# Fetching a batch's expert rows beside the attention rounds, and a routing chain spread over more gates: a two-layer transformer on one core

## What is computed

```
x = x + L0_attn(layernorm(x))   # differential attention, 16 heads of 8
x = x + L0_ffn(layernorm(x))    # 8 experts of 512, top 2 of 8, capacity 1280 rows an expert
x = x + L1_attn(layernorm(x))   # causal attention, 16 heads of 64
x = x + L1_ffn(layernorm(x))    # 8 experts of 64, top 4 of 8, and a shared one of 256
```

## Time and profile before

| | |
|---|---|
| median of 3 runs | 1513.7 us (1513.47 to 1518.37) |
| the profiled execution | 1500.44 us, span 1499.2 us |
| PE busy | 1437.6 us, 96% of the span |
| DVE, ACT, POOL busy | 1074.6, 951.5, 745.5 us |
| mean granted PE clock | 0.994 of full speed |

### The profile page before, as it was taken

The page is one execution under the profiler, slowest core; times in us unless marked ns, Lnnn a source line. Parts: engine busy times, 40 slices in busy tenths (PEclk is TensorE's granted clock), DMA queues, the critical chain, the costliest instruction groups (busy, mean ns, idle before and its releaser), DMA issues.

```text
span 1499.2 us, 26266 instructions
## 1 busy us (share of the span) xinstructions
PE 1437.6 (96%) x8801; PEld 856.5 (57%) x8801; DVE 1074.6 (72%) x3430; ACT 951.5 (63%) x2448; POOL 745.5 (50%) x1260
## 2 busy tenths in 40 slices
PE   4999999999989999979999999999999999998999
PEld 2434443444438889855565655656565565655666
DVE  5899999999944777547677687777767777674333
ACT  4588888887884334436767677676767777673221
POOL 7334656665455633633636365454636444353322
PEclk9999999999999999989999999999999999999999
DMA  7266655556334665720000000000000000020421
GB/s 142 57 159 134 143 141 148 110 106 150 113 131 165 213 211 190 256 64 1 15 1 15 1 12 5 3 14 1 16 2 14 3 1 2 2 58 1 99 76 52
DMA packets 70600, 113.39 MB, mean 76 GB/s; under 512 B 18857, under 2 KB 35114, under 8 KB 70458
## 3 DMA queue, kind: packets, MB, share of 16 engines
q0 software_dynamic: 33104, 61.73, 16.9%
q1 hardware_dynamic: 36928, 49.19, 10.9%
q10 hardware_dynamic: 434, 0.79, 0.2%
HBM read 71.86 MB, written 39.91 MB: 75 GB/s over the span
## 4 chain that ended last, share of the span: by engine, by line
PE 79%; DVE 10%; ACT 6%; issue 2%; POOL 1%; DMA 1%; SPq 0%; ACTq 0%; DVEq 0%; POOLq 0%
PE pS L1391 10%; PE bank L1424 9%; PE bank L1404 8%; PE bank L1235 6%; PE pS L1206 4%; PE bank L1433 4%; PE pS L1310 4%; PE bank L1376 4%; PE bank L1324 4%; PE bank L1361 4%; PE pS L1311 4%; PE bank L1372 3%; DVE mx L1831 3%; ACT ar L1561 3%; PE bank L1472 3%; PE bank L1226 2%
## 5 line engine op out<-in xcount | busy, mean ns | idle before, releaser
L2535 POOL TENSOR_SCALAR ar<-ar,rd 128x512 f32<-128x512 f32 (+3 forms) x512 | 269.3, 540 | 325.9 <-DVE rd L2266 324.0
L1831 DVE TENSOR_REDUCE mx<-pS 128x1 f32<-128x512 f32 x512 | 326.3, 677 | 19.4 <-PE pS L1206 17.6
L1651 ACT ACTIVATE ar<-ar,nm 128x512 f32<-128x512 f32 (+3 forms) x512 | 285.9, 560 | 83.1 <-DVE nm L2257 82.4
L2257 DVE CUSTOM_DVE_ANT_0 ar<-pS,maskf 128x512 f32<-128x512 f32 (+3 forms) x512 | 227.3, 481 | 6.3 <-PE pS L1391 4.4
L1561 ACT ACTIVATE ar<-bank 128x512 f32<-128x512 f32 x342 | 194.1, 598 | 44.8 <-PE bank L1226 41.6
L1404 PE MATMUL bank<-identr,all_r 128*128 128x128 f32 x1280 | 211.4, 287 | 4.6 <-DVE ar L2273 2.5
L1206 PE MATMUL pS<-all_r 64*128 64x512 f32 x512 | 205.7, 477 | 5.6 <-DVE mx L1831 4.7
L1404 PEld LDWEIGHTS bank<-identr,all_r 128*128 128x128 f32 x1280 | 134.3, 140 | 108.1 <-issue 83.4
L1661 ACT COPY ar<-bank 128x512 f32<-128x512 f32 (+3 forms) x256 | 107.4, 419 | 110.3 <-PE bank L1404 108.2
L1391 PE MATMUL pS<-ar 64*128 64x512 f32 (+3 forms) x1024 | 172.9, 456 | 0.8 <-DVE ar L2248 0.8
L1206 PEld LDWEIGHTS pS<-all_r 64*128 64x128 f32 x512 | 85.3, 192 | 127.7 <-DVE mx L1831 110.3
(11 more groups left out here) (306 smaller groups left out, 2638.2 us busy)
## 6 DMA issues: line engine op xcount, KB each, us to landing
rows_in<-zrow SPq DMA_DIRECT2D x16, 1024.0 KB, 5.3
ar<-gd SPq DMA_DIRECT2D x16, 512.0 KB, 6.7
all_r<-dk POOLq DMA_DIRECT2D x56, 128.0 KB, 3.7
dk<-xT SPq DMA_DIRECT2D x21, 256.0 KB, 3.6
dq<-xT SPq DMA_DIRECT2D x16, 256.0 KB, 5.0
rows_out<-ar SPq DMA_DIRECT2D x32, 128.0 KB
all_r<-dq POOLq DMA_DIRECT2D x28, 144.0 KB, 3.8
all_r<-dq POOLq DMA_DIRECT2D x28, 128.0 KB, 3.4
```

The costliest lines, as they stand in the source:

```text
L1651: S.activation(p, p, ACT.Exp, bias=nm1[:, c:c + 1], scale=-1.0, accum_out=den1[:, c:c + 1]).then_inc(*s_e1.inc(u, a))
L1831: V.tensor_reduce(mx[Gr % 2][:, col:col + 1], bS[n % 3], AX.X, ALU.max, negate=True).then_inc(*s_mx.inc(Gr, c))
L2257: V.tensor_tensor_reduce(pr_[pi][:, 0:w], pS[u % 2][:, 512 * a:512 * a + w], maskf[:, 512 - w:512], -0.125, 3e38, ALU.add, ALU.min, accum_ ...
L2535: G.tensor_scalar(p, p, rd1[:, c + a:c + a + 1], 1.0, ALU.mult, ALU.mult).then_inc(*s_p1.inc(u, a))
```

## The change

Batch 1's fetches leave `begin()` and go into `returned(1)`, so they stand in the C0 and C1 slots of rounds 0 to 3 and the combines in rounds 4 and 5. Batch 1's normalisation moves from rounds 2 and 3 to 6 and 7, its turn from round 5 to round 7, and its eight value projections from rounds 6 to 16 to one a round in rounds 8 to 15. `last_route()` is spread over gates 0 to 16 instead of 0 to 10, with batch 6's weights first.

```
     def returned(b):
-        if b != 1:
-            yield from fetched(b)
+        yield from fetched(b)
...
         for a in range(2):
             add("heads", 0, 0, a)
             yield
-        yield from fetched(1)
...
-        if k == 5 and b + 1 < NB:
+        if k == (5 if b else 7) and b + 1 < NB:
             add("turn1", b + 1)
...
-            if k + late in V1_AT and 0 < to < NB:
-                n = V1_AT.index(k + late)
+            times = V1_AT if to > 1 else V1_SECOND
+            if k + late in times and 0 < to < NB:
+                n = times.index(k + late)
                 add("v1", to, n // 2, n % 2)
...
-        if k == 2 and b + 1 < NB:
+        if k == (2 if b else 6) and b + 1 < NB:
             add("ln", "c", b + 1)
-        if k == 3 and b + 1 < NB:
+        if k == (3 if b else 7) and b + 1 < NB:
             add("apply", "c", b + 1)
...
     def last_route():
+        def gates(n):
+            for _ in range(n):
+                yield
+
         add("op1", NB - 1)
-        yield
+        add("weigh1", NB - 2)
+        yield from gates(1)
         add("ln", "d", NB - 1)
-        yield
+        yield from gates(2)
+        add("gturn", NB - 2)
         add("apply", "d", NB - 1)
-        yield
+        yield from gates(2)
         add("rturn1", NB - 1)
-        yield
+        yield from gates(2)
         add("logits", "d", NB - 1)
-        yield
+        yield from gates(2)
         add("likely", "d", NB - 1)
         add("bias", NB - 1)
+        yield from gates(1)
         add("top", "d", NB - 1)
-        yield
         add("chosen", "d", NB - 1)
-        yield
-        for b in (NB - 2, NB - 1):
-            add("weigh1", b)
-            yield
-            add("gturn", b)
-            yield
+        yield from gates(3)
+        add("weigh1", NB - 1)
+        yield from gates(3)
+        add("gturn", NB - 1)
+        yield
 
     V1_AT = (6, 8, 10, 12, 13, 14, 15, 16)
+    V1_SECOND = tuple(range(8, 16))
```

More of the change, by code:

```diff
@@ L567, in last_route @@
     def last_route():
+        def gates(n):
+            for _ in range(n):
+                yield
         add("op1", NB - 1)
-        yield
+        add("weigh1", NB - 2)
+        yield from gates(1)
         add("ln", "d", NB - 1)
-        yield
+        yield from gates(2)
+        add("gturn", NB - 2)
         add("apply", "d", NB - 1)
-        yield
+        yield from gates(2)
         add("rturn1", NB - 1)
-        yield
+        yield from gates(2)
         add("logits", "d", NB - 1)
-        yield
+        yield from gates(2)
         add("likely", "d", NB - 1)
         add("bias", NB - 1)
+        yield from gates(1)
         add("top", "d", NB - 1)
-        yield
-        add("chosen", "d", NB - 1)
-        yield
-        for b in (NB - 2, NB - 1):
-            add("weigh1", b)
-            yield
-            add("gturn", b)
-            yield
+        add("chosen", "d", NB - 1)
+        yield from gates(3)
+        add("weigh1", NB - 1)
+        yield from gates(3)
+        add("gturn", NB - 1)
+        yield
     V1_AT = (6, 8, 10, 12, 13, 14, 15, 16)
+    V1_SECOND = tuple(range(8, 16))
     back = returned(1)
```

## The result

| | before | after |
|---|---|---|
| median, 4 runs each | 1514.28 us (1513.47 to 1518.37) | 1497.32 us (1496.42 to 1498.29) |
| the profiled execution, its span | 1500.44, 1499.2 us | 1496.64, 1495.1 us |
| PE busy, mean granted clock | 1437.6 us, 0.994 | 1438.5 us, 0.997 |

The ratio is 0.9892 [0.987, 0.9914]: 17.0 us less by the medians, where 17.5 were forecast (1496.2 us). But the two profiled executions lie only 3.8 us apart, so the traces can't be compared as wholes. I cut them at places that both have, and read the start of each piece from PE's timeline.

The account below looks back on a forecast made before the run. PE was taken to bound the kernel, so only its waits and low clock could pay. -11.5 + 0.9 + 1.3 - 8.2 = -17.5 us, from 1513.7 to 1496.2 us; range 1492 to 1503, the forecast's own 1493.5 to 1499.

Parts of the forecast that it names:

- part 1: Start of the rounds: without batch 1's combine ahead in DVE's queue, round 1's scores come 11.5 us sooner.
- part 2: Rounds 0 to 3: batch 1's eight spread fetches cost nothing; without cover by projections 8.6 us in all.
- the rule: Skill page: GpSimd's DMA issue blocks while VectorE holds their shared port; would cost up to 20 us; slower rival 4%.
- part 3: Round 4: two combines ahead of DVE's maximum delay it some 1.15 us, of which 0.9 reach PE.
- part 4: Round 7: batch 1's turn, in the round of its normalisation, makes PE wait 1.3 us.
- part 5: Rounds 8 to 15: batch 1's value projections, one a round, cost nothing, as PE's work is unchanged.
- part 6: Gates of the last routing: the new order removes PE's waits and slower work, saving 8.2 us.

Follow-up runs that it names:

- the fill: The kernel before, with nine extra matmuls (result unused) ahead of the keys, to keep PE busy in its 8.67 us wait: 1500.44 us, ratio 0.9993 to before.
- combine moved: The kernel before with the start's change, but batch 1's fetches left in `begin()` and the last routing as before: 1498.5 us, ratio 0.9978 to before.
- weights early: The kernel before, with only batch 6's gate weights computed right behind the projection and turned ahead of the logits: median 1502.57 us, ratio 0.9994 to before.
- combines apart: The change, with batch 1's fetches one a step, combines spread so no round holds two, turn in round 8: 1484.34 us, ratio 0.9863 to before; later 1487.72 us.
- before, again: The kernel before, unchanged, profiled once more: 1512.12 us.

## Why the prediction was right

**The start (part 1, -11.5): right, -11.17.** Queries to keys was forecast at 1.7 us and is 1.97; round 0 to 1 takes 9.04. The wait was DVE's combine behind fetched rows, since moving the combines alone takes it away. The split, 8 for the wait and 3.6 for the clock, holds as a sum. But the fill shows that the clock is not simply tied to the long wait: without it 1.9 of the 3.6 us came back.

**The fetches (part 2, 0): the price right, the reading of the rule not.** No wait for the scaling appears in rounds 0 to 3. Without the spread it costs 3.3 us, by combine moved. The moved fetches took 0.95 to 1.08 us, all 64 at most 1.107, beside a busy DVE. The 3100 ns of the Trainium skill (SBUF — State Buffer, section on SBUF's two separate sides) is seen at none of them. But the page gives as the cause an operation of VectorE in a mode with two ports, which a 32-bit copy from SBUF to SBUF triggers, and the copies that ran beside the fetches here read a bank of PSUM (L2253, L2278). So I read too much into rows 8 when I took them as speaking against the rule: they only show that the neighbours which these fetches have cost next to nothing. The longest fetch is the one at 715.11, which began beside the last 0.16 us of an operation from SBUF to SBUF (L1777, from 713.60 for 1.67 us). No run here puts the page's case to the test.

**The double combine (part 3, +0.9): right in kind, too small.** The wait is 1.28 us, and round 4 grows by 1.21. The maximum starts 2.70 us behind the scores, where an even round had 1.16: a delay of 1.54, less the slack of 0.27, is 1.27. I had put the delay at 1.15, from a pair of combines that took 1.29; these took 1.71 (695.97 to 697.68).

**The turn (part 4, +1.3): right.** The wait is 1.14 us. By rounds it is 1.35: round 7 grows by 1.69, and round 5, where the turn stood, shrinks by 0.34.

**The value projections (part 5, 0): the step that failed.** "PE's work is unchanged" is true and not enough. In an even round a projection partly fills a gap that PE has anyway (0.61 us), in an odd one it adds its whole pitch (0.93). Rounds 6 and 16 lose one and shrink by 0.62 each, rounds 9 and 11 gain one and grow by 0.93 and 0.92: +0.61 us. With it 1.21 + 1.35 + 0.61 = 3.17, and round 1, 0.25 shorter, makes it the measured 2.92. In round 1 of before PE waited 0.18 us for DVE's copy of a projection (L2239), and that wait is gone.

**The last routing (part 6, -8.2): -7.94.** The turn does wait, for 0.29 us, where I had none. Batch 6's weights are about half of the gain (3.81 us, by weights early), batch 7's longer way is the other. Against executions with the old order in which the clock stays low for longer behind one of the two waits (46.16 to 47.05 us), it saves 9.3 to 10.2.

**The sum.** -17.5 was forecast, the pieces give -16.2, the medians -17.0. I carried the saving over to a median that stood 13.3 us above the profiled execution, with no reason for the gap. A part of the reason is now seen: the profiled execution had an early start, and executions with a late one take 8 to 12 us more. The rest is open: the other times of the kernel before in that comparison, 1513.5 to 1518.4 us, lie above the late ones of other chips (1510 to 1512.6), and no trace of them was kept. Of the change's four, two have a mean clock of 0.997 and are as late as the two with 0.978 and 0.982. In the one that was profiled, 6.0 of the 12.0 us were lost by 461 us, mostly in a wait of 1.64 us at 442 and at the low clock behind it. The other 6.0 were lost later, at full clock: from 470 us on PE's waits sum to 7.2 us there, and to 2.6 in the first trace of before. So the clock is less than half of that late start, and why PE waited more is open. The nearness of 1497.3 to 1496.2 owes something to luck: the medians' difference depends on how many executions of either kernel are late, and by how much. Two of PE's rows in that trace, one of either kind:

```profile
442.21 0.78 PE L1231 MATMUL bank<-all_r 64*128 64x512 f32 x1 [1.64 <-ACT ar L1566]
...
535.10 0.40 PE L1341 MATMUL bank<-rr,onesf 128*128 128x24 f32 x2 [1.70 <-DVE rr L2158]
```

## What to carry to other kernels

Before a transfer's consumer is moved out of an engine's queue, look at what else the transfer's issuer has behind it: the combine and the fetches had to move together, or 3.3 of the 11.2 us would have gone back to a wait for POOL. Work of the same size is dearer in a round in which its engine has no gap (0.93 against 0.61 us here), and dearer still where another tenant of its bank is not read out yet (1.53 to 1.64); price a move by the round's length with and without it. Where executions of a kernel differ by 10 us, cut the traces at common places: pieces of 80 to 600 us agree within 0.15 us here and show 0.3 us that no median does. And where a profiled execution lies 13 us from the median, profile the kernel once more before a saving is carried over: the first trace may show the rarer kind of execution.

## What the hardware did that I had not expected

**The end of the first layer's attention does not take the same time in every execution of one program.** In the traces with round 0 at 658.0 to 658.5 us the clock from 425 to 450 is 1.00; with 0.93 it is at 658.7 to 659.4, with 0.86 at 660.5, and with 0.54 to 0.55 at 666.8 to 667.6. In between, the clock fell at the same place but came back: in combines apart it is 0.52 from 427 to 430 us and 1.00 from 433 to 436. The profiled execution of after, with 0.85 and 669.99, does not fit this row: its clock fell later, at 442 us, and half of its delay came behind 461 us at full clock (see the sum above). PE's timeline of the first trace of before:

```profile
425.88 0.23 PE L1214 MATMUL bank<-identr,mp 128*32 128x128 f32 x1 [1.62 <-POOL mp L2426]
...
429.07 1.10 PE L1235 MATMUL bank<-ar 128*32 128x512 f32 x8
```

The same kernel again:

```profile
425.65 0.23 PE L1214 MATMUL bank<-identr,mp 128*32 128x128 f32 x1 [1.61 <-POOL mp L2426]
...
429.44 1.93 PE L1235 MATMUL bank<-ar 128*32 128x512 f32 x8
```

The same program, the same wait, 1.62 and 1.61 us; behind the one PE runs on at 2.4 GHz, behind the other at 1.2 (the window from 425 to 450 has 0.54, the next 25 us 0.91). The rounds begin 9.1 us later. What decides it stays open; I did not try to fill that stage.

**Two smaller places do the same.** From round 127 to gate 0 takes 10.5 us in ten traces and 12.0 to 12.2 in three, in combines apart with the clock at 0.69 from 1340 to 1345 us. And in before, again, the 2.86 us wait for `xs` is followed by the window below, where it was followed by full clock in the first trace. By gate 8 that has cost 4.6 us; 2.4 of them come back from there to gate 13, where the wait for batch 6's weights is shorter (2.12 instead of 3.05 us) and the clock does not fall behind it. The change takes this last place away: its gates took 36.82 to 36.92 us in seven traces.

```profile
1380.00:1385.00 5.00, 4.83 (x13) 2.77 (x13) 0.71 (x2) 1.09 (x2) 1.27 (x1) 0.50 0.00 0
```
